# One exact iteration in place of two in a chunked scan, with the check and the order of a turn rewritten

## What is computed

```python
def _mlp(params, h):
    W1, b1, W2, b2 = params
    return jax.nn.silu(h @ W1 + b1) @ W2 + b2
def loss_fn(params, k_t, v_t):
    return jnp.mean((_mlp(params, k_t) - v_t) ** 2)
def step(params, kvt):                      # one token of both sequences
    k_t, v_t = kvt
    g = jax.grad(loss_fn)(params, k_t, v_t)
    return tuple((p - LR * gp for p, gp in zip(params, g))), None
params, _ = jax.lax.scan(step, (W1, b1, W2, b2), (k, v))   # 1024 steps
return _mlp(params, q)
```

## Time and profile before

| | |
|---|---|
| three runs | 482.81, 483.13, 485.10 us (median 483.13) |
| the profiled execution, own time | 484.08 us |
| its span, first to last instruction | 481.9 us |
| PE busy, whole span | 430.7 us (89%) |
| POOL busy, whole span | 243.1 us (50%) |
| the 16 turns | from 177 to 326 us of the span |
| a steady turn | 9.29 us |
| PE, DVE, ACT, POOL busy in it | 9.22, 6.74, 5.41, 5.12 us |

### The profile page before, as it was taken

The page is one execution under the profiler, slowest core; times in us unless marked ns, Lnnn a source line. Parts: engine busy times, 40 slices in busy tenths (PEclk is TensorE's granted clock), DMA queues, the critical chain, the costliest instruction groups (busy, mean ns, idle before and its releaser), DMA issues.

```text
span 481.9 us, 9866 instructions
## 1 busy us (share of the span) xinstructions
PE 430.7 (89%) x2875; PEld 356.0 (74%) x2875; DVE 280.8 (58%) x1031; ACT 245.1 (51%) x617; POOL 243.1 (50%) x369
## 2 busy tenths in 40 slices
PE   7899899999908989999999999999799799999940
PEld 5444699999903679899999989974644499999930
DVE  4945455555528646677777777754965245555514
ACT  3594355555410445556556565544696145555520
POOL 4367777545500344555555546552247777554530
PEclk9799999999957999999999999999989999999985
DMA  8981334100075200000000000000001417110028
GB/s 231 260 278 56 113 104 151 37 26 25 18 186 175 41 1 0 3 2 2 1 2 1 1 2 2 3 0 1 2 23 56 112 50 205 35 34 28 20 63 216
DMA packets 34513, 30.89 MB, mean 64 GB/s; under 512 B 3838, under 2 KB 30085, under 8 KB 34464
## 3 DMA queue, kind: packets, MB, share of 16 engines
q1 hardware_dynamic: 24608, 19.17, 14.7%
q0 software_dynamic: 4544, 8.47, 5.4%
q10 hardware_dynamic: 5312, 2.62, 2.1%
HBM read 15.55 MB, written 15.61 MB: 65 GB/s over the span
## 4 chain that ended last, share of the span: by engine, by line
PE 73%; DVE 8%; DMA 6%; POOL 4%; issue 4%; ACT 4%; ACTq 0%; SPq 0%; DVEq 0%; POOLq 0%
PE bank L1308 18%; PE bank L741 15%; PE bank L728 14%; POOL slots_dram L1435 3%; PE bank L599 3%; DMA stage<-y_dram 3%; PE bank L1101 2%; PE bank L689 2%; PE bank L716 2%; PE bank L1178 2%; DMA stage<-slots_dram 2%; PE bank L1139 1%; DVE stats L419 1%; PE bank L699 1%; PE bank L1162 1%
## 5 line engine op out<-in xcount | busy, mean ns | idle before, releaser
L1692 DVE TENSOR_TENSOR sq<-bank,relu 128x512 f32<-128x512 f32 x86 | 59.5, 692 | 84.2 <-ACT relu L839 84.0
L1440 POOL DMA_INDIRECT y_dram<-y_out,stage x78 | 76.9, 986 | 59.2 <-ACT y_out L865 52.6
L741 PE MATMUL bank<-proj_w,sq 128*128 x624 | 86.4, 281 | 2.8 <-DVE sq L1692 2.8
L728 PE MATMUL bank<-tileT,tile_w 128*128 128x128 f32 x624 | 83.2, 277 | 0.0
L1435 POOL DMA_INDIRECT slots_dram<-rows,slots x64 | 63.3, 990 | 35.0 <-DVE slots L535 15.2
L741 PEld LDWEIGHTS bank<-proj_w,sq 128*128 128x128 f32 x624 | 75.6, 191 | 6.5 <-issue 3.5
L839 ACT ACTIVATE relu<-bank 128x512 f32<-128x512 f32 x94 | 56.1, 596 | 45.4 <-PE bank L728 37.6
L728 PEld LDWEIGHTS bank<-tileT,tile_w 128*128 128x128 f32 x624 | 76.9, 195 | 0.0
L865 ACT ACTIVATE y_out<-bank,stage 128x128 f32<-128x128 f32 x78 | 28.7, 368 | 33.2 <-PE bank L741 33.2
L1303 POOL TENSOR_TENSOR sq<-sq,last_rows 128x128 f32<-128x128 f32 x32 | 14.7, 458 | 54.2 <-DVE sq L1279 54.2
L599 PE MATMUL bank<-ones 128*128 128x512 f32 x32 | 20.6, 790 | 15.4 <-DVE res L1743 12.6
(11 more groups left out here) (278 smaller groups left out, 1046.6 us busy)
## 6 DMA issues: line engine op xcount, KB each, us to landing
slots_dram<-pad SPq DMA_DIRECT2D x2, 2535.0 KB, 14.0
stage<-slots_dram SPq DMA_DIRECT2D x18, 260.0 KB, 4.4
fc_w<-experts SPq DMA_DIRECT2D x1, 2048.0 KB, 20.3
proj_w<-experts SPq DMA_DIRECT2D x1, 2048.0 KB, 24.0
stage<-y_dram SPq DMA_DIRECT2D x8, 256.0 KB, 5.5
stage<-y_dram ACTq DMA_DIRECT2D x8, 256.0 KB, 6.2
y_dram<-y_out,stage POOLq DMA_INDIRECT x78, 2.3
res<-x SPq DMA_DIRECT2D x4, 256.0 KB, 3.8
```

Source lines behind the costliest of these rows:

```text
L728: last = nc.tensor.matmul(bank[i % 2][:, f_cols], tile_w[:, i % 2, f_cols], tileT[:, (f * NQ + tile_q(i)) % 2, tile_cols(i)], start=True, ...
L741: last = nc.tensor.matmul(bank[4 + i % 2][:, 0:P], sq[:, i % 2, f_cols], proj_w[:, k, f_cols], start=j == 0, stop=j == FJ - 1)
L1440: nc.gpsimd.indirect_dma_start(y_dram.ap(), bass.IndirectOffsetOnAxis(tiles[:, t, P:P + 1].bitcast(U32), 0), y_out[:, t % YBUFS, :], None, ...
L1692: nc.vector.tensor_tensor(wide_of(i)[2], wide_of(i)[0][:], wide_of(i)[1], ALU.mult)\
```

## The change

- `late` is one exact iteration instead of two. It starts from e1 of the turn before, as the first one did; the second one, with `ee` of the exact chain, is gone. `again` of the exact iteration takes both operands as f32.
- The check: the difference is now that of the exact iteration and the rounded e1 it started from (`gap_of_last`), and there is a new quantity: the squared difference of e0 and e1 (`gap_of_steps`, `square_steps`, `add_steps`, of the `d` half alone), 3 more operations of POOL per turn. The flag takes three more small operations of DVE after the loop.
- The orders of a turn on PE, DVE, ACT and POOL are new.

```diff
-            late, early = [], []
-            for r in range(ROUNDS):
-                late.append(Step(final, ROUNDS * turn + r, turn + r, turn, r, late[-1] if r else earlier, r == 0))
+            late, early = Step(final, turn, turn, turn, turn % KEPT, earlier), []
+            for r in range(AHEAD):
                 early.append(Step(ahead, n + r, n + r, turn + 1, 1 + turn % 2 if r else 0, early[-1] if r else None))
...
-            mm(x.h_bank, old.chain.ed[:, old.to, 1, :], old.chain.kk[:, step.block, :], start=False)\
+            mm(x.h_bank, as_kind(step, old.chain.ed[:, old.to, 1, :]), x.kk[:, step.block, :], start=False)\
...
+            def gap_of_steps(turn):
+                old, new = (0 if turn else 1), 1 + (turn + 1) % 2
+                pool.wait_ge(ahead.d_done, FIRST_AHEAD + AHEAD * turn)
+                nc.gpsimd.tensor_tensor(step_gap, ahead_ed[:, new, 1, :].bitcast(F32), ahead_ed[:, old, 1, :].bitcast(F32),
+                                        ALU.subtract).then_inc(step_gap_made, 1)
+            def square_steps(turn):
+                pool.wait_ge(step_gap_made, turn + 1)
+                nc.gpsimd.tensor_tensor(step_sq, step_gap, step_gap, ALU.mult).then_inc(step_squared, 1)
+            def add_steps(turn):
+                pool.wait_ge(step_squared, turn + 1)
+                nc.gpsimd.tensor_tensor(squares[:, 4, :], squares[:, 4, :], step_sq, ALU.add).then_inc(gap_done, 1)
+            def gap_of_last(turn):
+                pool.wait_ge(final.erows_done, turn + 1)
+                pool.wait_ge(final.d_done, turn + 1)
+                nc.gpsimd.tensor_tensor(gap, last_ed[:, turn % KEPT], ahead_ed[:, 1 + (turn + 1) % 2].bitcast(F32),
+                                        ALU.subtract).then_inc(gap_made, 1)
```

More of the change, by code:

```diff
@@ L55 @@
 PADS = 3
-TOL = 5e-5
+TOL = 1e-4
+GAP_LIMIT = 3e-3
 LR = 1e-3
@@ L1250, in act_erows @@
             act.wait_ge(x.et_done, step.n + 1)
[L1251 to L1255, removed]
+            if x is final and turn >= KEPT:
+                act.wait_ge(gap_made, turn - KEPT + 1)
+                act.wait_ge(new_squared, turn - KEPT + 2)
+            if x is ahead and step.to and turn >= 1:
+                act.wait_ge(gap_made, turn)
             nc.scalar.copy(x.ed[:, step.to, 0, :], x.t_bank[:, 2 * P:3 * P]).then_inc(x.erows_done, 1)
@@ L1291, in dve_ee @@
             x = step.chain
[L1292 to L1298, removed]
+            dve.wait_ge(x.da_done, step.n + 1)
+            nc.vector.tensor_tensor(x.ee[:, step.to, :], x.d_bank[:, 0:P], mask, ALU.mult).then_inc(x.ee_done, 1)
         def pool_slope(pool, step):
@@ L1466, in square_new @@
             def square_new(turn):
+                new = last_ed[:, (turn - 1) % KEPT]
                 nc.gpsimd.tensor_tensor(new_sq, new, new, ALU.mult).then_inc(new_squared, 1)
@@ L1482, in _ @@
                 late, early = turn_steps(turn)
+                gap_of_steps(turn)
                 if turn:
                     square_gap(turn)
[L1485 to L1488, removed]
+                pool_slope(pool, late)
+                square_steps(turn)
                 if early:
@@ L1491, in _ @@
                 if turn:
-                    add_new(turn)
[L1493 to L1497, removed]
+                    add_gap(turn)
+                    square_new(turn)
+                add_steps(turn)
+                if early:
+                    pool_slope(pool, early[1])
+                if turn:
+                    add_new(turn)
+                gap_of_last(turn)
             for part in (square_gap, add_gap, square_new, add_new):
@@ L1554, in _ @@
                     act_silu(act, early[1], turn)
-                act_rows(act, late[1])
+                act_erows(act, late, turn)
                 if early:
@@ L1949, in _ @@
                 more = early and before
[L1950 to L1953, removed]
+                if before and not early:
+                    pe.wait_ge(ahead.erows_done, before[1].n + 1)
+                pe_first(pe, late, turn)
                 if more:
                     pe_w1_sums(pe, before[1], ahead_upd1)
+                    pe_b1_sums(pe, before[1], ahead_upd1)
+                pe_again(pe, late)
+                if more:
                     pe_w2_sums(pe, before[1])
-                pe_offset(pe, late[0], turn)
-                if more:
-                    pe_b1_sums(pe, before[1], ahead_upd1)
                     pe_w2t_sums(pe, before[1], ahead_upd2)
[L1961 to L1964, removed]
+                pe_offset(pe, late, turn)
+                pe_old_guess(pe, late)
                 if early:
@@ L1969, in _ @@
                     pe_first(pe, early[0], turn)
-                pe_y(pe, late[0], turn)
-                pe_th_transposed(pe, late[0])
-                pe_first(pe, late[1], turn)
+                pe_aa(pe, late, turn)
+                pe_a_transposed(pe, late, turn)
+                pe_yrows(pe, late, turn)
+                pe_y(pe, late, turn)
                 if early:
+                    pe_aa(pe, early[0], turn)
+                    pe_y(pe, early[0], turn)
                     pe_offset(pe, early[0], turn)
-                    pe_aa(pe, early[0], turn)
@@ L2008, in _ @@
-                if early:
-                    pe_th_transposed(pe, early[1])
-                pe_e_transposed(pe, late[1])
-                if early:
+                    pe_y(pe, early[1], turn)
+                    pe_yrows(pe, early[1], turn)
+                    pe_th_transposed(pe, early[1])
+                pe_w1_sums(pe, late, upd1_done)
+                pe_b1_sums(pe, late, upd1_done)
+                pe_w2_sums(pe, late)
+                if early:
+                    pe_inner(pe, early[1])
```

145 lines of the change are left out of this document (56 added, 89 removed).

## The result

The change made the kernel slower: 488.45 us (median of 20 runs, 484.30 to 494.08) against 483.77 (20 runs, 482.47 to 485.62), a ratio of 1.0089 with a 95% interval of 1.0064 to 1.0114. The prediction was 479.3, with a range of 469 to 489, and the chance it gave to "slower" was 0.25.

What follows compares the result with a forecast made beforehand. The ring of dependencies through all engines, not PE's work, was taken to bound the kernel. 15 turns at 0.22 us less (3.3) and 0.5 at the end made 3.8 us less: 479.3 us, range 469 to 489.

Steps and rivals of the forecast that it cites:

- The ring: Dependencies of the two rounded iterations through all engines, in three links a turn: 9.28 us before the change.
- link 1: From `da` of e1 to silu of the next e0: 2.72 us before, forecast 2.14, a gain of 0.58.
- The walk: Pricing the three links in the new order: 2.14 + 4.50 + 2.43 = 9.07 us a turn, 0.22 less.
- the upper hand-over: Delay of a hand-over to PE: 0.05 at the least, 0.15 at the most; the forecast took 0.07.
- The wait for POOL: In silu of e0 to silu of e1, `d` of e0 waits 0.51 us for POOL's slope of e0.
- The square that no row showed: POOL's 128x128 square_steps between the two slopes: taken as 0.39 us, bounds 0.31 and 0.46.
- rival 4: The granted clock falls in the scan: some 489 us if every second turn, 498 if every turn; chance 0.11.
- the sum: Total of the forecast: 15 turns x 0.22 = 3.3 us, with 0.5 at the end, 3.8 us less.
- The end of the scan: Last turn and POOL's sums for the check: 0.9 us won, less added reduction and DVE work, taken as 0.5.
- Rivals 1 and 3: Rival 1: POOL is no wait for `d`, a turn of 8.56 us, some 472 us, chance 0.18; rival 3 follows.
- rival 3: Six hand-overs to PE in the ring take 0.15, not 0.07: turn 9.55, some 486 us, chance 0.24.
- Rival 2: PE is the bound: the turn falls by 1.73 to 7.56 us, the time to some 457 us; chance 0.05.

Runs made afterwards that it cites:

- e0: Not a run: the first of the two rounded iterations in a turn of the scan; no time of its own as a kernel.
- Experiment 1: Changed kernel plus six unread two-pass matmuls a turn where TensorE waits (first late, again e1, aa e1): 481.71 us, ratio 0.9948 to the kernel before.
- experiment 4: Changed kernel plus two wide unread matmuls while TensorE waits for the check's sums after the loop: 488.48 us, ratio 1.0096 to the kernel before.
- e5: Changed kernel plus one unread two-pass matmul a turn, ahead of again e1: 480.68 us, ratio 0.9947 to the kernel before.
- e9: Changed kernel plus one unread two-pass matmul a turn, behind first late: 490.5 us, ratio 1.0076 to the kernel before.
- e10: Changed kernel plus one unread two-pass matmul a turn, ahead of inner e0: 482.61 us, ratio 0.9975 to the kernel before.

## Why the prediction was wrong

**The ring and its links held, with link 1 too short.** The walk gave 2.14, 4.50 and 2.43, a turn of 9.07; at full clock it is 2.30, 4.49 and 2.37, a turn of 9.16. Link 1 is off by 0.16 because w1_sums started 0.15 behind `ee`, the upper hand-over, and not 0.07, and PE then took 0.92 to first e0, not 0.83. The wait for POOL was forecast as 0.51 and is 0.49 (253.83 - 252.93, against the 0.41 of the walk). The square that no row showed took 0.41, forecast 0.39. So the steady turn gained 0.13 and not 0.22. Without the half clock the 14 turns would be 3.0 us shorter than before (128.24 and 131.26), and the forecast's 14 x 0.22 is 3.1, but that they agree is luck: 1.2 of the 3.0 are the two long turns behind the fall before, which the forecast took to stay. Experiment 1 shows the kernel with the clock held: 0.5% faster, where the prediction had 0.8%.

**The step that failed is rival 4, the clock, which the sum put at nothing.** It cost 10.3 us in the profiled execution. It was named, and the price of a fall was good: some 1.2 us, and a turn with one takes 10.33 - 9.16 = 1.17 more. That its 489 us with a fall in every second turn came so near to the median of 488.45 is in part luck: the falls come in two groups and not in every second turn, and the execution with seven long turns took 490.58. It got a chance of 0.11 by the argument that the emptiest 2 us of a turn would have PE busy for 1.4, while 1.19 in 2 us at the end of the scan had stayed at 1.00. The emptiest 2 us of the new turn have 1.36, as forecast, and the clock fell all the same, right behind them:

```profile
200.00:202.00 2.00, 1.36 (x10) 1.02 (x9) 0.85 (x4) 0.69 (x4) 2.00 (x5) 1.00 0.02 4
202.00:204.00 2.00, 2.00 (x11) 1.98 (x12) 0.92 (x5) 0.74 (x3) 0.43 (x2) 0.61 0.00 0
```

One row of the trace in which the clock had held was no bound. It was a single occasion, and a turn comes 15 times; in the 20 runs the mean clock goes from 0.911 to 0.934 and the time with it, 494.08 us at 0.914 and 484.30 at 0.933. What I should have seen is that the change takes from PE 1.7 of 7.9 us of passes while the ring stays as long, so that PE must wait more, longest behind `da` of e0 (0.51 us); and the trace of before had shown what can follow when PE runs short, in turn 0 itself. The rows agree: a window inside a long turn reads 0.50 (236 to 240 us), turns of 9.16 us read 1.00, and the values between are those of windows that hold both.

**The end of the scan** was forecast 0.5 us shorter and came out 0.8 longer, by the same step: the sums end 1.16 earlier (10.63 and 11.79, forecast 0.9), but then the query's matmuls ran at half clock, which costs 1.55 up to the first row of the result (experiment 4), and the longer sum and verdict 0.4. Over the whole rest of the span, 164.5 us against 164.1 before, the loss is 0.4, since before the clock fell behind that row (0.91 over the 20 us from 334.84, in the changed kernel 1.00 over those from 342.07).

**Rivals 1 and 3.** That POOL is no wait is refuted: moving one line gives 0.36 us a turn. Hand-overs of 0.15 were met in two places of the ring (w1_sums and inner of e0: 251.92 to 252.07), and 0.05 or 0.06 in the other four, so rival 3 has a part of the 0.09 by which the turn is longer than forecast, and no more. Rival 2, PE as the bound, is refuted by experiment 1: 12 passes more in a turn change nothing.

**Open:** why the clock falls in some turns and not in others that look the same. All 14 falls begin right behind the stretch from inner e0 to aa e1, which fits that a fill inside or just ahead of it helps and one behind first late doesn't, but what of that stretch decides isn't shown. The emptiest 2 us of a turn are 1.58 us busy in e5, where no turn fell, and 1.36 in both e9 and e10, where three falls and one came, so that measure doesn't tell these two apart (rows of e5, e9 and e10):

```profile
184.84:186.84 2.00, 1.58 (x12) 1.23 (x11) 1.76 (x10) 0.56 (x2) 1.38 (x3) 1.00 0.00 0
```

```profile
183.22:185.22 2.00, 1.36 (x9) 1.03 (x9) 0.77 (x4) 0.77 (x4) 1.09 (x3) 1.00 0.00 0
```

```profile
182.98:184.98 2.00, 1.36 (x9) 1.03 (x9) 0.77 (x4) 0.77 (x4) 1.08 (x3) 1.00 0.00 0
```

## What to carry to other kernels

A change that takes work off TensorE and leaves the ring of dependencies as long can lose by it: TensorE waits more, the clock can fall, and a pass then takes twice as long (here 0.21 us, from 308.56 to 308.77, for 0.11). Look for the wait that grows, here a side job put ahead of an operation of the ring on an in-order engine, and move the side job rather than fill the wait; where it can't be moved, an unread matmul in the right place can hold the clock. Measure what such a fill wins on the whole span: at the end of the scan it only moved the fall. Price a clock that may fall by all places of that kind in the loop, not by one row in which it held.

## What the runs showed of the hardware that was not expected

Two passes (0.22 us) a turn, ahead of again e1, hold the granted clock at 1.00 over the scan, where without them it is 0.89 on the mean; the same two passes some 3.5 us later in the turn, behind first late, leave it at 0.94 with four long turns in 14. All 14 falls in the turns of the changed kernel and of what was made from it begin 5.0 to 5.5 us behind a silu of e0, though TensorE's single waits ahead of them are no longer than about 0.5 us between its rows (0.7 between weight loads). Two wide unread matmuls in a wait at the end of the scan moved a fall to a later stretch and left the span as long. On POOL, an operation that doesn't need the one ahead of it starts 0.05 us before that one's recorded end (252.90 against 252.95), so slope, square and slope take 1.23 us (252.49 to 253.72) and not the 1.33 of their rows.
